# A decoder layer on one core: the last group's first expert stage on rows sorted by expert, and its attention six slots nearer

## What is computed

```python
# x: (16, 128, 128); flat: (2048, 128)
ssm_out = scan over 128 steps, 16 states a feature          # first stage
routing = softmax(flat @ Wr + br); top1_w, top1_i = max, argmax of routing   # 4 experts
hid     = silu(einsum('nd,edf->enf', flat, up_w) + up_b[:, None, :])         # f = 512
all_out = einsum('enf,efd->end', hid, down_w) + down_b[:, None, :]
out     = ssm_out + all_out[top1_i[n], n] * top1_w          # one expert of the four counts
x = x + layernorm(out)
x = x + attention(layernorm(x), ctx_512)                    # one head, 128 keys
x = x + second_mixture(layernorm(x))   # top 2 of 8, tokens numbered in order, silu, 512 hidden
```

## Time and profile before

| what | value |
|---|---|
| median of 3 runs | 481.47 us (481.04 to 482.59) |
| the profiled execution's own time | 482.02 us |
| its span, first to last instruction | 480.2 us |
| busy: PE, DVE, ACT, POOL | 344.7, 292.0, 263.0, 230.6 us |
| granted TensorE clock, mean | 0.885 of full |
| read from HBM, written | 13.73 MB, 10.52 MB |

### The profile page before, as it was taken

One profiled execution on the slowest core, in us unless ns is written; L12 is line 12 of the kernel. 1 busy time (PEld: TensorE's weight loads), 2 busy tenths in 40 slices (PEclk: granted clock), 3 DMA queues, 4 the chain that ended last, 5 costly groups with the idle time before them and its releaser, 6 DMA issues. The chain is left out here.

```text
span 480.2 us, 5947 instructions
## 1 busy us (share of the span) xinstructions
PE 344.7 (72%) x1749; PEld 233.6 (49%) x1749; DVE 292.0 (61%) x840; ACT 263.0 (55%) x465; POOL 230.6 (48%) x275
## 2 busy tenths in 40 slices
PE   1427557769896899978999688661537789999460
PEld 0203333346464565645667455561327757767360
DVE  3478988956999799999974245357136012222055
ACT  3554645668887797868537675413224474554021
POOL 4425755543545665464541422716844435455434
PEclk9999965879999899999899988975558899999966
DMA  6999400000000000000000000200120221210243
GB/s 123 290 233 333 124 1 1 0 0 1 1 1 0 2 1 1 1 2 0 1 1 2 0 0 9 81 1 23 50 61 28 77 67 49 76 53 14 78 120 88
DMA packets 29472, 23.94 MB, mean 50 GB/s; under 512 B 5448, under 2 KB 23943, under 8 KB 29440
## 3 DMA queue, kind: packets, MB, share of 16 engines
q1 hardware_dynamic: 27048, 19.50, 14.8%
q0 software_dynamic: 2304, 4.04, 2.5%
q10 hardware_dynamic: 88, 0.03, 0.0%
HBM read 13.73 MB, written 10.52 MB: 51 GB/s over the span
## 5 line engine op out<-in xcount | busy, mean ns | idle before, releaser
L1072 POOL TENSOR_TENSOR yD<-yD,hc 128x512 f32<-128x512 f32 x64 | 84.4, 1318 | 103.5 <-DVE hc L537 97.9
L1398 PE MATMUL bank<-yD,w 128*128 128x512 f32 x128 | 71.9, 645 | 17.1 <-ACT hid L1202 16.2
L502 DVE TENSOR_TENSOR_SCAN h<-a,bank 128x512 f32<-128x512 f32 x64 | 77.8, 1216 | 1.4 <-DVE bank L489 0.5
L1407 PE MATMUL bank<-w,hid 128*128 128x128 f32 x512 | 74.6, 293 | 0.0
L1407 PEld LDWEIGHTS bank<-w,hid 128*128 128x128 f32 x512 | 68.6, 205 | 9.4 <-issue 6.1
L1389 PE MATMUL bank<-rows,selid 99*128 99x512 bf16 x128 | 47.5, 457 | 25.5 <-DVE hc L537 23.4
L1135 POOL DMA_INDIRECT y_rows<-yslot,dest x40 | 39.1, 977 | 37.6 <-DVE yslot L865 22.1
L1202 ACT ACTIVATE hid<-bank,cols 128x512 f32<-128x512 f32 x64 | 43.4, 683 | 18.0 <-PE bank L1398 11.9
L489 DVE TENSOR_TENSOR bank<-bank,u 128x512 f32<-128x512 f32 x64 | 43.8, 684 | 14.5 <-PE bank L1389 14.2
L1060 POOL DMA_INDIRECT slots_in<-xrow,posu x32 | 32.3, 1010 | 32.7 <-DVE locs L684 14.7
L1389 PEld LDWEIGHTS bank<-rows,selid 99*128 99x128 bf16 x128 | 12.8, 106 | 67.4 <-DVE hc L537 47.0
(11 more groups left out here) (235 smaller groups left out, 586.4 us busy)
## 6 DMA issues: line engine op xcount, KB each, us to landing
slots_in<-yslot SPq DMA_DIRECT2D x10, 258.0 KB, 6.3
xe_tok<-slots_in SPq DMA_DIRECT2D x8, 258.0 KB
y_rows<-yslot SPq DMA_DIRECT2D x8, 256.0 KB, 5.2
x_tok<-in_x_dram SPq DMA_DIRECT2D x4, 256.0 KB, 3.9
w<-in_L_attn_up_w_dram SPq DMA_DIRECT2D x1, 1024.0 KB
yD<-y_rows SPq DMA_DIRECT2D x4, 256.0 KB, 4.4
xT<-y_rows SPq DMA_DIRECT2D x4, 256.0 KB, 5.7
out_dram<-acc SPq DMA_DIRECT2D x4, 256.0 KB, 2.3
```

The source lines that it names most:

```text
L502: ins = v.tensor_tensor_scan(state_of(k), decay_of(k).rearrange("p j n -> p (j n)"), drive_of(k), 0.0, ALU.mult, ALU.add)
L1072: pool.tensor_tensor(grp(yD, g), grp(yD, g), read_of(k), ALU.add).then_inc(summed, 1)
L1398: pe.matmul(bank[UP_BANKS[f % 2]][:, 0:width(g)], w1[:, e, f * P:(f + 1) * P], grp(yD, g), start=True, stop=True).then_inc(up_ps, 1)
L1407: ins = pe.matmul(bank[DOWN_BANK][:, j * P:(j + 1) * P], hid[:, m % 2, f, j * P:(j + 1) * P], w2[:, e, f, :], start=(f == 0), stop=(f == F ...
```

## The change

Groups 0 to 2 keep the dense stage (`dense_at`). For group 3 (`DENSE`) the four experts no longer run on all tokens. DVE numbers the tokens by expert (`choose_expert`, `sort_places`), each expert's rows rounded up to whole tiles of 128, which makes at most 4 + 4 - 1 = 7 tiles (`MT`). POOL scatters the 4 tiles of rows to `srt_in` in DRAM, SP loads them back as 7 tiles, PE transposes them. `sort_owners` works out which expert owns each tile; SP reads the number into a register and fetches that expert's two weight matrices (256 KB each) from DRAM for each tile, into a ring of four. Each tile gets 4 matmuls of 128x128 up, `silu3`, and 4 down. The outputs go to `srt_out`, and POOL gathers them back in token order with 4 indirect DMAs (`rows_back`, slot 78). DVE adds them in `add_rows` in slot 79.

The attention of group 3 begins at slot 80 where it was 86 (`LAST_LAG = 16`); `FIRSTS_SLOT` stays 86. The second choices are now sent 2 in slot 88 and 10 in slot 90. The diff, cut (declarations, the expert's bias by tile, and the transposes and counts on PE are left out):

```diff
...
+DENSE = G - 1
+MT = GT + E1 - 1
+W_RING = E1
+FULL = GT
...
+def dense_at(k, step):
+    g = mix_at(k, step)
+    return g if g != DENSE else None
...
+LAST_LAG = 16
...
-        if k == NS * (g + 1) + 22 + at_step:
+        if k == NS * (g + 1) + (22 if g < G - 1 else LAST_LAG) + at_step:
...
-SECONDS_PARTS = {SECONDS_SLOT + 1: range(0, 2), SECONDS_SLOT + 3: range(2, 10), FIRSTS_SLOT + 9: range(10, 12)}
+SECONDS_PARTS = {SECONDS_SLOT + 1: range(0, 2), NS * G + LAST_LAG + LATE_STEPS[14]: range(2, 12)}
...
-LAST_SLOT = NS * G + 22 + LATE_STEPS[22]
-EARLY_SLOT = NS * G + 22 + LATE_STEPS[20]
+LAST_SLOT = NS * G + LAST_LAG + LATE_STEPS[22]
+EARLY_SLOT = NS * G + LAST_LAG + LATE_STEPS[20]
+CHOOSE_SLOT, COUNT_SLOT, SORT_SLOT, ROWS_SLOT, TURN_SLOT, TILE_SLOT, BACK_SLOT, ADD_SLOT = 66, 67, 68, 69, 72, 73, 78, 79
...
+def ups_at(k):
+    return [j for j in range(2 * (k - TILE_SLOT), 2 * (k - TILE_SLOT) + 2) if 0 <= j < MT]
...
+def downs_at(k):
+    done = [j - 1 for j in ups_at(k) if j]
+    return done + [MT - 1] if MT - 1 in ups_at(k) else done
...
+HALVES = ((0, GT), (GT, MT))
...
+                do(v.tensor_copy(oh1_bf[:], oh1[:]))
...
+            def sort_places():
+                v.wait_ge(cnt_ps, 1)
...
+                link(v.tensor_reduce(count1[:], tot.rearrange("p i e -> p e i"), AX.X, ALU.add))
+                link(v.tensor_tensor(full[:], count1[:].unsqueeze(2).to_broadcast(room),
+                                     rows128[:].unsqueeze(1).to_broadcast(room), ALU.is_gt))
...
+                link(v.tensor_tensor(off1[:], off1[:], cum, ALU.add))
+                at["cnt"] = n[0]
+                link(v.tensor_tensor(off1[:], off1[:], oh1[:], ALU.mult))
+                link(v.tensor_reduce(spos[:], off1[:], AX.X, ALU.add))
+                link(v.tensor_copy(sposu[:], spos[:]))
+                at["spos"] = n[0]
...
+            def sort_owners():
...
+                link(v.tensor_copy(owner_no[:], owner[0:1, :]))
+                at["owner"] = n[0]
...
+            def add_rows():
+                g = DENSE
+                v.wait_ge(gathered, 16 * GT)
+                v.wait_ge(init_done, g + 1)
+                for j, i in enumerate(tiles_of(g)):
+                    do(v.scalar_tensor_tensor(acc[:, i, :], back[:, j, :], rz[:, 0, i:i + 1], acc[:, i, :],
+                                              ALU.mult, ALU.add))
+                at["acc", g, E1 - 1] = n[0]
...
-                    if (g := mix_at(k, 4 * e + 9)) is not None:
...
+                if k == CHOOSE_SLOT:
+                    choose_expert()
+                if k == SORT_SLOT:
+                    sort_places()
+                if k == ROWS_SLOT:
+                    sort_owners()
+                    gate_first(DENSE)
+                if k == ADD_SLOT:
+                    add_rows()
...
-            sp.wait_ge(up_ps, G * E1 * FT)
+            load(srt_in[0:GW, :].rearrange("(p r) d -> p r d", p=P), blank[:, :, 0:P], cleared)
+            load(srt_in[GW:MT * P, :].rearrange("(p r) d -> p r d", p=P), blank[:, 0:MT - GT, 0:P], cleared)
...
+            def weights(j):
...
+                r = j % W_RING
+                e = sp.value_load(owner_no[0:1, j:j + 1], min_val=0, max_val=E1 - 1)
+                if j >= W_RING:
+                    sp.wait_ge(dn3_ps, j - W_RING + 1)
+                load(w1[:, r, :], up_w[bass.ds(e, 1), :, :].rearrange("e d f -> d (e f)"), ld_wt[r])
+                load(w2[:, r, :, :], down_w[bass.ds(e, 1), :, :].rearrange("e (t p) d -> p (e t) d", p=P), ld_wt[r])
+            def rows_out(half):
+                lo, hi = HALVES[half]
+                sp.wait_ge(evicted, half + 1)
+                load(srt_out[lo * P:hi * P, :].rearrange("(j p) d -> p j d", p=P), ys[:, lo:hi, :], st_rows)
...
+            sp.wait_ge(dve_done, at["owner"])
+            sp.wait_ge(dn_ps, downs(DENSE - 1, E1))
+            for j in range(W_RING - 1):
+                weights(j)
+            sp.wait_ge(sorted_in, 16 * GT)
+            load(xs_tok, srt_in[:].rearrange("(j p) d -> p j d", p=P), ld_rows)
+            for j in range(W_RING - 1, MT):
+                weights(j)
+            for half in range(2):
+                rows_out(half)
+            sp.wait_ge(dn3_ps, MT)
             sp.dma_start(fb_b, fc2_b.rearrange("(o e) d -> o e d", o=1).broadcast_to([P, E2, P])).then_inc(ld_fb, 16)
             sp.wait_ge(scattered, 16 * 2 * START[G - 1])
+            sp.wait_ge(xs_ps, 1)
             sp.dma_start(xe_early[:], slots_in[0:LATE0, :].rearrange("(e p) d -> p e d", p=P)).then_inc(ld_early, 16)
             sp.wait_ge(scattered, 16 * 2 * TILES)
+            sp.wait_ge(st_rows, 32)
...
+            def sort_rows():
...
+                pool.wait_ge(yraw_done, 1)
+                pool.wait_ge(dve_done, at["spos"])
+                for j in range(GT):
+                    pool.indirect_dma_start(srt_in[:], bass.IndirectOffsetOnAxis(ap=sposu[:, j:j + 1], axis=0),
+                                            yraw[:, j, :], None, bounds_check=MT * P - 1,
+                                            oob_is_err=False).then_inc(sorted_in, 16)
...
+            def rows_back():
+                pool.wait_ge(st_rows, 32)
+                for j in range(GT):
+                    pool.indirect_dma_start(back[:, j, :], None, srt_out[:],
+                                            bass.IndirectOffsetOnAxis(ap=sposu[:, j:j + 1], axis=0),
+                                            bounds_check=MT * P - 1, oob_is_err=False).then_inc(gathered, 16)
...
+                if k == ROWS_SLOT:
+                    sort_rows()
+                if k == BACK_SLOT:
+                    rows_back()
...
+            def silu3(j):
+                act.wait_ge(up3_ps, j + 1)
+                if j == 0:
+                    act.wait_ge(dve_done, at["up_bias"])
+                    act.wait_ge(dn_ps, downs(DENSE - 1, E1))
+                for f in range(FT):
+                    ins = act.activation(hid_of(j, f), bank[UP_BANKS[j % 2]][:, f * P:(f + 1) * P], ACT.Silu,
+                                         bias=up_bias[:, j, f:f + 1])
+                ins.then_inc(hid3_done, 1)
...
+            def take_out(half):
+                lo, hi = HALVES[half]
+                act.wait_ge(dn3_ps, hi)
+                act.activation(ys[:, lo:hi, :], tiles3(bank[DOWN_BANKS[half]][:, 0:(hi - lo) * P]), ACT.Copy
+                               ).then_inc(evicted, 1)
...
                                     w2[:, e, f, :], start=(f == 0), stop=(f == FT - 1))
                 ins.then_inc(dn_ps, 1)
+            def up3(j):
+                pe.wait_ge(xsT_done, half_of(j) + 1)
...
+                if j >= 2:
+                    pe.wait_ge(hid3_done, j - 1)
+                else:
+                    pe.wait_ge(hid_done, DENSE * E1 * FT)
+                for f in range(FT):
+                    ins = pe.matmul(bank[UP_BANKS[j % 2]][:, f * P:(f + 1) * P], w1[:, j % W_RING, f * P:(f + 1) * P],
+                                    xsT[:, j, :], start=True, stop=True)
+                ins.then_inc(up3_ps, 1)
...
+            def down3(j):
+                b = DOWN_BANKS[half_of(j)]
+                o = bank[b][:, j % GT * P:(j % GT + 1) * P]
+                pe.wait_ge(hid3_done, j + 1)
+                if j == 0:
+                    pe.wait_ge(dve_done, at["acc", DENSE - 1, E1 - 1])
+                if j == GT:
+                    claim(b, (evicted, 2))
+                for f in range(FT):
...
+                    o = claim(MIX_BANK, (dve_done, at["cnt"]))
...
+                    flat = oh1_bf[:].rearrange("p i e -> p (i e)")
...
+                        if done == j - 1 or done == j == MT - 1:
+                            down3(done)
             def turn_early():
```

113 lines of the change are left out of this document (108 added, 5 removed).

## The result

The changed kernel takes 509.62 us (median of 4 runs, 507.35 to 509.71), the kernel before took 482.03 beside it (4 runs, 481.04 to 484.96): a ratio of 1.055, 95% interval 1.0495 to 1.0606. It is slower by 27.6 us. The forecast was 500, so the size is short by 9.6 us, and the time lies 0.6 us above the upper end of the range of 488 to 509 (the kernel before took 0.56 us more beside it than the 481.47 from which the forecast started).

The account below looks back on a forecast made before the run. It took the early rows' arrival, not matmuls, as the bound: group 3's sum at 319.2 plus 57.9 gives 377.1, 17.9 later than 359.2; span 498.1, profiled 499.9, forecast 500 us, range 488 to 509.

Parts of the forecast that it names:

- What the change removes: Group 3's dense stage: matmuls fall from 32 units to 14, 16 us of TensorE less.
- rival D: Faster: early rows' arrival follows the matmuls, so 16 us less gives 466 us; needs group 3's sum by 301.3; chance 0.06.
- 16 us less at equal clock: Sign expected in the changed profile: TensorE's busy time some 16 us less at equal clock.
- Up to the sum: Group 3's router, sorting, tile matmuls and gathers: its sum ends at 319.2 us, only 2.4 earlier than 321.6.
- A - R: From the start of group 3's first router matmul to the end of group 3's sum on DVE: forecast 62.4 us.
- the sorted rows are hidden here: Behind group 2's normalization: last sort scatter lands by 276.5 us, the load ends at 280.5, before normalization ends at 285.7.
- From the sum to the early rows: From group 3's sum to the early rows' load: instruction order makes it 57.9 us, against 37.6 before.
- Everything ahead of R: Before group 3's router matmuls: two DVE constants and two clearing stores near the start, costed at nothing.
- The tail: From the early rows' arrival to the end of the span: 121.0 us, order left alone by the change.
- rival B: Shorter tail: shifted order meets neither unnamed wait, 4.39 and 3.17 us, so 492 us; chance 0.17.
- Rival C: Low clock in the whole ladder of sorted-tile matmuls: 10 us more, 510 us; chance 0.12, slow weight fetches included.

Follow-up runs that it names:

- less dense kernel: The kernel before, with 12 of group 3's 32 units of dense matmuls left out and nothing of the change: 475.65 us, ratio 0.9888.
- the two runs that brought the rows sooner: The changed kernel without fetches of weights by register (508.98 us), and the changed kernel with sorted rows loaded ahead of all weight fetches (508.04 us).
- the ladder ahead: The changed kernel with the sorted tiles' matmul ladder one slot earlier (TILE_SLOT 72): 501.71 us, ratio 1.0403.
- Lag 22: The changed kernel with group 3's attention lag back at 22, second choices sent as before, add_rows in slot 85: 497.14 us, ratio 1.0352.
- seconds ahead: The changed kernel with all twelve second-choice scatters ahead of group 3's third inverse root: 503.92 us, ratio 1.046.
- all repairs: The changed kernel with LAST_LAG 19, ladder slot 72, sorted rows loaded first, FIRSTS_SLOT two sooner, ADD_SLOT 80, second choices behind first: 490.62 us, ratio 1.0173.
- rows first: The changed kernel with the load of the sorted rows ahead of all seven tiles' weight fetches on SP: 508.04 us, ratio 1.0538.

## Why the prediction was right, and where it was off

The direction and the two places of the loss, the round trips and the order behind the sum, were right; the size was short by 9.6 us, and of what holds group 2 back only one of three holds was named. By the prediction's own steps:

- **What the change removes**, 16 us of TensorE. True of the work, but overpriced from the start as a gain: the less dense kernel got half of such time back. So rival D, faster, was further away than its argument suggests: with 12 units out and no round trips, the sum still ended at 314.8, with group 2's logits ahead in the same queue, and D needed it by 301.3. TensorE's busy time fell by only 6.7 us (344.7 to 338.0), but with a granted clock of 0.820 in place of 0.885, so the sign of "16 us less at equal clock" can't be read.
- **Up to the sum**: forecast A - R 62.4, measured 68.8. This term was mis-sized by 6.4 us. Its front was exact: the sort scatters started 13.4 us after R, as planned (270.2 - 256.8; measured 272.96 - 259.54), and the last ended 18.5 after it, against 18.6. Then, each relative to R: the first silu's end 2.0 late, the seventh's another 2.7, the last down at the low clock 1.2, the store 0.5 (3.1 us from the end of the eviction to the first gather, where the sum has 2.5); eviction, gathers and the sum itself came as forecast. The recorded sum is 0.6 us more than its terms here (307.5 + 0.9 + 0.6 + 2.3 is 311.3 and not 311.5, and three steps of 1.27 and 2.3 more end at 317.6 and not at 318.0), which only helped it. What failed first is the sentence "the sorted rows are hidden here": the last scatter took 4.43 us to land, where I had taken 2.28 from the earlier trace rows, with the load behind fetches in SP's queue. But the two runs that brought the rows sooner gained only 1 us of first up, since group 2's transposes, for which TensorE then waits 1.2 us, and the bias sums at the low clock (6.4 us with them, from 286.66 to 293.04) stand ahead. The run with the ladder ahead shows where it really lay: 6.2 us went with the bias sums, two table loads and four exponentials out of the way. I had those in the sum at their price; I had not asked whether they need stand there, nor what the low clock does to a last down behind 4.16 us of idleness.
- **From the sum to the early rows**: forecast 57.9, measured 58.5, and right step by step: group 2's statistics end at A+2.6 as forecast, group 3's row maximum at A+23.2 (23.5), the sixth scatter at A+34.4 (34.3), and the tenth of the last ten starts at A+51.8 (51.7). Lag 22 puts the same stretch back to 37.8, so its length is the order's. The single culprit I named first, though, `add_rows` ahead of `add_attention`, is worth only 3 us by itself: the same delay is in force on GpSimd (gathers ahead of the root), and both come on top of the 12 us by which group 2's attention is late beside the ladder, which the forecast did not name. Larger than the addition are the ten bare scatters (4.0 alone) and, by the trace, `places` behind the row maximum: 6.0 us lie between the end of the one-hot cast (345.46) and `places` (351.49). That part was not tested alone, and group 2's count stands behind group 3's scores on TensorE too (350.64).
- **Everything ahead of R** was costed at nothing and came 2.7 us later. The two constants take 0.4 on DVE, but at group 0's router matmuls nothing of it is left (81.70 us, 81.89 before). 2.1 arise between the router matmuls of group 0 and those of group 1, and 0.8 before group 2's. Those of groups 0 and 1 are 56.6 us apart in both traces without the change and in one with it (seconds ahead), 57.1 to 58.8 in the others. The granted clock from 150 to 200 us was 0.97 in these three traces and 0.93 in the others. Between the two traces without the change R differs by as much, 2.1 us, though they are the same ahead of it. With one trace of each kernel, cause and effect can't be told apart; this stays open.
- **The tail** of 121.0 measured 120.9, and rival B fell: the unnamed wait is there again, 4.66 us at 396.37, behind a silu as before, with a second one of 1.84 at 402.19 where 3.17 had been.
- **Rival C**: the ladder ran at the full clock (1.06 us a group at 301.82, 2.4 GHz), only its first two ups (3.78 for two groups) and its last down (2.07) at the low one, 1.2 GHz. Of its 10 us only the last down's 1.2 came, since the forecast had the first ups at the low clock already. That the measured time lies at C's 510 is chance. The Trainium skill's "TensorE: Matmul & The Clock Gate", under "HAM oscillation — how this bites in real kernels", warns that bursts of matmuls parted by long waits for data start at half clock each time. The trace agrees at both ends of the ladder, where TensorE had waited 8.94 and 4.16 us; inside it, where its waits were under 1 us, no group behind the first down (1.48) ran low.

In sum, the 27.6 us between the two spans are 2.7 ahead of R, 4.0 up to the sum, and 20.9 behind it. Up to the sum, the last down ends 6.1 us sooner after R than in the kernel before (57.5 against 320.4 - 256.8 = 63.6), for 16 us of matmuls less, and the way back through DRAM takes more than that (11.3 us from the last down's end to A, where it was 1.2). Of the 24.9 us by which R to E grew, the lag alone gave back 10.1 and all repairs 19.0: these are order, of group 3's attention and of the ladder. The kernel before is still 5.9 us shorter there (102.4 against 108.3); that group 2's attention stands behind the ladder is what the traces show of this rest, and no run took it away.

## What to carry to other kernels

Price a removed matmul only up to the next wait in its own queue: about half of what was taken out here hung on another group's step that stood ahead in the same queue. When a change makes one value arrive in another way (a gather in place of a sum), list, for each engine, what stands behind the instruction that waits for it; here the same delay stood in two queues, and mending one of them gave 3 us of 21. When moving steps to fill a gap, move the tiny ones (a count of 0.26 us) as carefully as the big ones: one of them behind a waiting matmul cost 5 us. And when a run is cut at a moment that the change itself moves, as the sum here, read the stretch across it as well: lag 22 looked like 20.7 us won behind the sum, and 10.7 of them had only moved ahead of it.

## What the runs showed of the hardware

- A scatter of 128 rows, 0.97 us to issue, landed 2.28 us after its start in the kernel before, and 4.43 us where six fetches of 256 KB were issued on SP in the 4 us around it (274.9 to 279.0). With no fetches ahead of the load (rows first), SP issued it 2.3 us after the last scatter had started, and the sorted rows were turned 23.4 us after R in place of 25.6.
- Fetches addressed by a register landed in 3.8 us (up) and 4.5 us (down) for 256 KB, near the 4.0 of the input loads of that size, and leaving them out changed nothing that can be measured.
- A gather of 128 rows from DRAM took 1.00 us to issue and 2.6 us to land; the forecast had used a scatter's 0.97 and 2.28.
